# Two cross-attention layers with layer norm: d spread by two transfers through DRAM, the variance from ScalarE's squares, x's blocks in 4 transfers, new orders of work

## The reference

```
q = x Wq + bq          k = ctx Wk + bk          v = ctx Wv + bv
w = softmax over the 224 rows of x of (q k^T / sqrt(512))
y = w v + x
out = (y - mean(y)) / sqrt(var(y) + 1e-6) * gamma + beta       (over the 512 columns)
```

## Time and profile before

| What | Value |
|---|---|
| median of 3 runs | 1051.82 us |
| profiled execution | 1052.02 us, span 1050.1 us |
| PE busy | 1013.1 us, 96% of the span |
| PEld busy | 950.3 us, 90% |
| DVE busy | 867.4 us, 83% |
| ACT busy | 668.7 us, 64% |
| POOL busy | 563.3 us, 54% |
| DMA queue of SP | 99.02 MB, 43.8% of 16 engines |
| bv_row load on SP, issue to landing (median of 2) | 5.0 us |
| DVE waiting for the landing of cb before turn_ctx | 4 times, 2.4 us in all, longest 0.8 |
| ACT_TABLE_LOAD | once, 1.3 us |

### The profile page before, as it was taken

The page is one execution under the profiler, slowest core; times in us unless marked ns, Lnnn a source line. Parts: engine busy times, 40 slices in busy tenths (PEclk is TensorE's granted clock), DMA queues, the critical chain, the costliest instruction groups (busy, mean ns, idle before and its releaser), DMA issues.

```text
span 1050.1 us, 24861 instructions
## 1 busy us (share of the span) xinstructions
PE 1013.1 (96%) x6984; PEld 950.3 (90%) x6984; DVE 867.4 (83%) x2595; ACT 668.7 (64%) x1873; POOL 563.3 (54%) x517
## 2 busy tenths in 40 slices
PE   6888999999999999999999999999999999999984
PEld 5877999999999999999999999999999999999973
DVE  2465888888988888898898888998898889888864
ACT  2325676666666766767667766676677667666643
POOL 0013455665556556655556566555565665555653
PEclk9688999999999999999999999999999999999997
DMA  7743444444544443445444444454444444544101
GB/s 160 162 102 69 84 101 102 89 89 100 109 91 103 103 100 84 91 98 110 90 103 104 97 90 85 97 110 91 102 104 98 94 82 99 108 94 97 48 18 35
DMA packets 391214, 99.59 MB, mean 95 GB/s; under 512 B 324992, under 2 KB 375040, under 8 KB 391168
## 3 DMA queue, kind: packets, MB, share of 16 engines
q1 hardware_dynamic: 388528, 99.02, 43.8%
q10 hardware_dynamic: 2640, 0.01, 0.2%
HBM read 84.29 MB, written 14.68 MB: 94 GB/s over the span
## 4 chain that ended last, share of the span: by engine, by line
PE 91%; DVE 2%; issue 2%; POOL 2%; ACT 2%; SPq 1%; DMA 1%; POOLq 0%; DVEq 0%; ACTq 0%
PE oq_bank L599 26%; PE score_bank L575 8%; PE score_bank L576 8%; PE score_bank L580 8%; PE pv_bank L630 5%; PE pv_bank L625 5%; PE oq_bank L551 5%; PE pv_bank L626 5%; PE oq_bank L546 5%; PE oq_bank L547 5%; PE t_bank L511 3%; PE oq_bank L605 2%; PE pv_bank L457 1%; PE t_bank L528 1%; DMA y<-in_L_xattn_Wq_dram 1%
## 5 line engine op out<-in xcount | busy, mean ns | idle before, releaser
L599 PE MATMUL oq_bank<-probs,raw 125*128 125x224 f32 x1536 | 317.3, 357 | 5.2 <-ACT probs L766 5.2
L599 PEld LDWEIGHTS oq_bank<-probs,raw 125*128 125x128 f32 x1536 | 284.4, 192 | 7.7 <-ACT probs L766 3.6
L757 ACT ACTIVATE probs<-probs,neg_max 125x224 f32<-125x224 f32 x384 | 180.6, 471 | 141.9 <-DVE neg_max L967 141.8
L1151 POOL TENSOR_TENSOR psum<-probs 125x672 f32<-125x672 f32 x64 | 103.2, 1612 | 308.5 <-ACT probs L766 308.4
L575 PE MATMUL score_bank<-qT_hi,cT_hi 128*125 128x224 f32 x768 | 200.2, 287 | 3.0 <-ACT cT_hi L714 1.6
L576 PE MATMUL score_bank<-qT_hi,cT_lo 128*125 128x224 f32 x768 | 189.8, 273 | 0.0
L766 ACT ACTIVATE probs<-probs,rsum 125x224 f32<-125x224 f32 x384 | 153.3, 471 | 14.2 <-DVE rsum L975 12.7
L1194 POOL TENSOR_TENSOR y_out<-z,gamma_row 112x512 f32<-112x512 f32 x62 | 93.3, 1525 | 115.6 <-ACT z L790 115.6
L575 PEld LDWEIGHTS score_bank<-qT_hi,cT_hi 128*125 128x125 f32 x768 | 145.9, 190 | 7.4 <-issue 2.9
L580 PE MATMUL score_bank<-qT_lo,cT_hi 128*125 128x224 f32 x768 | 147.3, 273 | 0.0
L576 PEld LDWEIGHTS score_bank<-qT_hi,cT_lo 128*125 128x125 f32 x768 | 146.1, 190 | 0.0
(11 more groups left out here) (100 smaller groups left out, 2078.6 us busy)
## 6 DMA issues: line engine op xcount, KB each, us to landing
raw<-in_ctx_dram SPq DMA_DIRECT2D x64, 375.0 KB
cb<-in_ctx_dram SPq DMA_DIRECT2D x256, 92.0 KB
xb<-in_x_dram SPq DMA_DIRECT2D x512, 28.0 KB, 1.7
x<-in_x_dram SPq DMA_DIRECT2D x32, 448.0 KB, 3.6
out_dram<-y_out SPq DMA_DIRECT2D x31, 448.0 KB, 6.5
cb<-in_ctx_dram SPq DMA_DIRECT2D x128, 3.5 KB
y<-in_L_xattn_Wq_dram SPq DMA_DIRECT2D x2, 512.0 KB, 5.3
Wq_next<-in_L_xattn_Wq_dram SPq DMA_DIRECT2D x2, 512.0 KB, 5.8
```

The source lines that it names most:

```text
L599: ins = nc.tensor.matmul(o, raw[0:MP, u.slot, c, cols], probs[0:MP, u.par4, c, :], start=(c == 0), stop=(c == MC - 1))
L757: ins = act.activation(probs[0:MP, u.par4, c, :], probs[0:MP, u.par4, c, :], ACT.Exp, bias=neg_max[0:MP, u.par4, c:c + 1], scale=-1.0, acc ...
L1151: pool.tensor_tensor(psum3[0:MP, :, :], probs[0:MP, u.par4, 0:HALF, :], probs[0:MP, u.par4, HALF:MC, :], ALU.add).then_inc(psum3_done, 1)
```

## The change

The change has five parts.

- `spread_d` leaves TensorE and `d_out` leaves ScalarE. On SP, `save_d` writes `d_col` (112 partitions by 2 values of 4 bytes) to a DRAM tensor `d_kept`, and `spread_d` reads it back to 125 partitions of `d_row`, 224 values on each, when the first transfer has landed. `d_col` and `d_row` have two buffers, by parity of the unit.
- The mean is taken from the sum that `add_pv` now gives as a by-product (tensor_tensor_reduce); `minus_mean` (VectorE) scales it; `squares` (ScalarE) squares y minus the mean with the sum as accumulator output; `add_eps` and `shift` work on these. bn_stats and bn_aggr are gone.
- `load_xb` has 4 transfers of 112 KB.
- `transpose_x` waits for the low parts of the unit before, not for d.
- The orders of all five engines are new. TensorE's turn now begins with `q_product(a(+0), 0)`. SP's turn begins with the d of the last `b`.

```diff
-        XB_DMAS, CB_DMAS = P // RB * EC, P // RB * (LC + 1)
+        XB_DMAS, CB_DMAS = P // RB, P // RB * (LC + 1)
...
-                blocks = x[u.batch()].rearrange("(c r) (k b s) -> b k r c s", r=RB, k=EC, s=RB)
+                blocks = x[u.batch()].rearrange("(c r) (k b s) -> b r k c s", r=RB, k=EC, s=RB)
                 for b in range(P // RB):
-                    for k in range(EC):
-                        sp.dma_start(xb[b * RB:(b + 1) * RB, k, :, :], blocks[b, k]).then_inc(xb_loaded, 16)
+                    sp.dma_start(xb[b * RB:(b + 1) * RB, :, :, :], blocks[b]).then_inc(xb_loaded, 16)
...
+            def save_d(u):
+                if not u.real:
+                    return
+                if u.past(-2):
+                    sp.wait_ge(d_done[u.layer], u.batch(16))
+                    sp.sem_inc(wait_alone, 1)
+                sp.wait_ge(dot_done, u.n(m=2))
+                sp.sem_inc(wait_alone, 1)
+                sp.dma_start(d_kept[u.par].rearrange("(h p) -> p h", h=TH), d_col[0:TP, u.par, :],
+                             allow_slow_non_contiguous=True).then_inc(d_saved[u.layer], 16)
+            def spread_d(u):
+                if not u.real:
+                    return
+                if u.past(-2):
+                    sp.wait_ge(smax_done, u.n(-2, 6))
+                    sp.sem_inc(wait_alone, 1)
+                sp.wait_ge(d_saved[u.layer], u.batch(16, 16))
+                sp.sem_inc(wait_alone, 1)
+                sp.dma_start(d_row[0:MP, u.par, :], d_kept[u.par].partition_broadcast(MP)).then_inc(d_done[u.layer], 16)
...
             def turn(i, j):                      # SP
                 a, b = units(i, j)
+                save_d(b(-1))
+                spread_d(b(-1))
+                if a(-1).later(0):
+                    load_ctx(a(-1), 1)
                 if a(+0).later(1):
                     load_cb(a(+0))
+                save_d(a(+0))
                 if a(+1).later(1):
                     load_xb(a(+1))
+                spread_d(a(+0))
+                store(b(-2))
+                if a(+0).later(0):
+                    load_ctx(a(+0), 0)
                 if a(+1).later(1):
                     load_x(a(+1))
-                if a(+0).later(0):
-                    load_ctx(a(+0), 0)
-                    load_ctx(a(+0), 1)
-                store(b(-2))
...
             def turn(i, j):                      # TensorE, as it is after
                 a, b = units(i, j)
+                if j is None and i == 0:
+                    transpose_weights(0); fold_weights(0); fold_c(0); fold_w(0)
+                q_product(a(+0), 0)
+                pv_product(a(-1), 0)
+                pv_product(a(-1), 1)
+                q_product(a(+0), 1)
+                if j is None and i == 0:
+                    transpose_weights(1)
+                o_product(b(-1), 0)
                 score_product(a(+0), 0)
+                score_product(a(+0), 1)
                 o_product(b(-1), 1)
                 transpose_x(b(+0), 0)
                 score_product(a(+0), 2)
                 if j is None and i == 0:
                     fold_beta(); fold_weights(1); fold_c(1); fold_w(1)
+                pv_product(b(-1), 0)
                 transpose_x(b(+0), 1)
+                pv_product(b(-1), 1)
                 q_product(b(+0), 0)
                 q_product(b(+0), 1)
                 o_product(a(+0), 0)
                 score_product(b(+0), 0)
                 score_product(b(+0), 1)
+                score_product(b(+0), 2)
                 o_product(a(+0), 1)
...
+            def squares(u, h):                   # ScalarE
+                act.wait_ge(mean_done, u.n(m=2, add=h - 1))
+                act.activation(square_junk[0:TP, :], y[0:TP, u.par, h, :], ACT.Square, bias=neg_mean[0:TP, u.par, h:h + 1],
+                               accum_out=square[0:TP, u.par, h:h + 1]).then_inc(square_done, 1)
...
+                dve.tensor_tensor_reduce(y[0:TP, u.par, h, :], pv_bank[h][0:TP, :], y[0:TP, u.par, h, :], 1.0,
+                                         0.0, ALU.add, ALU.add, y_sum[0:TP, u.par, h:h + 1]).then_inc(y_done, 1)
+            def minus_mean(u, h):                # VectorE
+                dve.wait_ge(y_done, u.n(m=2, add=h - 1))
+                dve.tensor_scalar(neg_mean[0:TP, u.par, h:h + 1], y_sum[0:TP, u.par, h:h + 1], -1.0 / E, None,
+                                  ALU.mult).then_inc(mean_done, 1)
```

More of the change, by code:

```diff
@@ L150, in build_xattn @@
         qT_lo = sb("qT_lo", [P, LC, T], F32R)
-        d_col = sb("d_col", [P, TH])
-        d_row = sb("d_row", [P, T])
+        d_col = sb("d_col", [P, 2, TH])
+        d_row = sb("d_row", [P, 2, T])
         dot_junk = sb("dot_junk", [P, E])
@@ L729, in xT_hi_part @@
                 act.activation(xT_hi[:, u.par, 2 * g:2 * g + 2, :], src, ACT.Identity).then_inc(xT_hi_done, 1)
-            def d_out(u):
-                if not u.real:
-                    return
-                act.wait_ge(d_ready, u.n())
-                if u.past(-1):
-                    act.wait_ge(smax_done, u.n(-1, 6))
-                act.activation(d_row[:, :], t_bank[0][:, 0:T], ACT.Identity).then_inc(d_done, 1)
             def q_hi(u, l):
@@ L1050, in turn @@
                 a, b = units(i, j)
-                shift(b(-2), 0)
-                score_max(b(-1), 2)
+                add_pv(b(-2), 0)
+                invert_sum(a(-1), 1)
+                q_lo(b(-1), 0)
+                dot(a(+0), 1)
+                q_lo(b(-1), 1)
+                add_pv(b(-2), 1)
+                minus_mean(b(-2), 0)
+                minus_mean(b(-2), 1)
+                xT_lo_part(a(+0), 0)
+                turn_x(a(+0), 1)
+                score_max(b(-1), 0)
+                score_max(b(-1), 1)
+                score_max(b(-1), 2)
+                add_eps(b(-2))
+                xT_lo_part(a(+0), 1)
+                score_max(b(-1), 3)
+                turn_ctx(a(+0), 0)
+                invert_sum(b(-1), 0)
+                shift(b(-2), 0)
+                score_max(b(-1), 4)
+                o_lo(a(-1), 0)
+                ctxT_lo(a(+0), 0)
+                score_max(b(-1), 5)
+                turn_ctx(a(+0), 1)
+                o_lo(a(-1), 1)
                 shift(b(-2), 1)
-                dot(a(+0), 0)
-                dot(a(+0), 1)
                 residual(a(-1), 0)
                 residual(a(-1), 1)
-                score_max(b(-1), 3)
-                invert_sum(b(-1), 0)
-                o_lo(a(-1), 1)
-                score_max(b(-1), 4)
-                score_max(b(-1), 5)
-                ctxT_lo(a(+0), 0)
+                ctxT_lo(a(+0), 1)
                 add_pv(a(-1), 0)
                 q_lo(a(+0), 0)
-                turn_ctx(a(+0), 1)
                 invert_sum(b(-1), 1)
-                half_moments(a(-1), 0)
+                minus_mean(a(-1), 0)
+                turn_ctx(a(+0), 2)
                 add_pv(a(-1), 1)
-                half_moments(a(-1), 1)
-                moments(a(-1), 0)
-                moments(a(-1), 1)
-                ctxT_lo(a(+0), 1)
+                ctxT_lo(a(+0), 2)
                 q_lo(a(+0), 1)
@@ L1076, in turn @@
                     WqT_out(1)
+                minus_mean(a(-1), 1)
                 add_eps(a(-1))
-                turn_ctx(a(+0), 2)
+                turn_ctx(a(+0), 3)
+                score_max(a(+0), 0)
                 shift(a(-1), 0)
-                o_lo(b(-1), 0)
-                shift(a(-1), 1)
-                ctxT_lo(a(+0), 2)
-                score_max(a(+0), 0)
-                turn_ctx(a(+0), 3)
-                score_max(a(+0), 1)
-                ctxT_lo(a(+0), 3)
+                shift(a(-1), 1)
+                score_max(a(+0), 1)
+                score_max(a(+0), 2)
+                ctxT_lo(a(+0), 3)
+                score_max(a(+0), 3)
+                o_lo(b(-1), 0)
+                dot(b(+0), 0)
+                dot(b(+0), 1)
+                invert_sum(a(+0), 0)
+                o_lo(b(-1), 1)
                 xT_lo_part(b(+0), 0)
-                o_lo(b(-1), 1)
-                score_max(a(+0), 2)
-                score_max(a(+0), 3)
+                residual(b(-1), 0)
+                score_max(a(+0), 4)
+                residual(b(-1), 1)
                 if j is None and i == -1:
@@ L1109, in turn @@
                 xT_lo_part(b(+0), 1)
[L1110 to L1129 removed]
+                dot(a(+1), 0)
             turns(dve, turn)
```

187 lines of the change are left out of this document (73 added, 114 removed).

## The result

The changed kernel takes 1421.2 us (median of 4 runs, 1418.5 to 1423.6); the kernel before took 1050.6 in the same session. Ratio 1.3536, 95% interval 1.3516 to 1.3555: 35% slower. The forecast was 1055, range 1043 to 1071.

What follows compares the result with a forecast made beforehand. It took TensorE's own instruction list to bound the middle and chains of waits the two ends. Sum: 1052.0 - 9.7 (middle) + 0 + 12.7 (start) + 0.3 (end) = 1055.3, say 1055 us; range 1043 to 1071.

Steps and rivals of the forecast that it cites:

- Part 1: TensorE in the steady turn: without the two spread_d, 0.32 us saved a turn, 9.7 us in all.
- Part 2: Other engines in the steady turn: nothing becomes late, cost 0, range 0 to +15 us; tightest place q_lo(b,0).
- rival D: Engines at q_lo(b,0): the 0.5 us of slack is not there, 0.25 us a turn, 1063 us; chance 0.18.
- Rival E: ScalarE: Square needs another function table than Exp, four table loads a turn, 1112 us; chance 0.03.
- Part 3: SP's list in the steady turn: save_d lands in 2.0 us, waits covered, cost 0, up to 4 us a turn.
- rival C: SP's turn becomes the bound: spread_d(b) waits for save_d ahead of load_cb, 1071 us; chance 0.14.
- Part 4: The start: first d behind the preamble's loads, fold_beta +16.1 us, some regained; net +12.7, range +3 to +20.
- D: At the start, the time when the first unit's d lands: 56 us, from 46 up to 64.
- B: Rival at the start: preamble packets run denser, d lands near 47, net start +3, 1045 us; chance 0.18.
- Part 5: The end: last d's round trip hidden, last normalisation's mean and square cost +0.3 us, range -1 to +3.

Runs made afterwards that it cites:

- the floor: The changed kernel with no transfer of d in any turn, d_row filled once from a weights row in the preamble: 1037.8 us, 0.9884 of the kernel before.

## Why the prediction was wrong, by its own steps

**Part 1 was right.** The floor without transfers has a turn of (815.15 - 108.63) / 24 = 29.44 us; the same orders with two spreads on TensorE have (825.92 - 110.44) / 24 = 29.81. The difference is 0.37 for the 0.32 of the sum, and the two ratios, 0.9884 and 0.9982, differ by 10.3 us for its 9.7. The 0.12 from there to the 29.93 before would be 3.6 us, within the 5 us by which the kernel before varies from run to run.

```profile
108.63 2.28 PE oq_bank L590 x12
...
815.15 2.28 PE oq_bank L590 x12
```

**Part 2 was right.** In the floor TensorE waits once in 840 us, for 0.4 us, so the slack that rival D doubted is there. The whole floor is 11.8 us under the kernel before, where parts 1 and 2 gave 9.7. Rival E falls too: the trace of the changed kernel has one ACT_TABLE_LOAD, and its squares take 719 ns.

**Part 3 failed**, at this sentence: no such write is in the trace, "so I bound save_d by these 1.6 and 7.3 and take 2.0, near the median, since the queue is almost empty then". The write lands after 7.1. The nearest row was of another kind: xb's transfers read DRAM in pieces of 128 bytes. The bounds of 1.6 and 7.3 hold the median, though not the longest landing, 10.3; taking a value near the low end took the loss out of the forecast. The reason given, an almost empty queue, is refuted by the lone write on an idle core, 5.9 to 6.9 us. The Trainium skill, "DMA: Bandwidth & Descriptors", section "Anatomy of one DMA — SWDGE (gpsimd) path", with its fixed 2.0 us, gives the same sum; the trace disagrees for this write (7.1, and 7.8 where GpSimd issues it), and the lone transfers lie on both sides of it (1.15 for one row, 6.7 for d).

The high end was too small as well. I had "up to 4 us a turn", and for rival C one us a turn for each us beyond 2.5. At 7.1 that makes 7.1 - 2.5 - 0.8 = 3.8 a turn, times 31 and on top of 1055, 1173 us; it was 11.3 a turn. What C left out: the length of cb's issues, 14.2 us on the chain where the sum has 9, by the load of ctx's columns now ahead of them, the read and the write; and TensorE's lower clock behind the wait, about 2 us. 3.8, 5.2 and 2 are 11.0 of the 11.3, an estimate, since its terms come from different turns. In whole kernels the read was worth 83 us and the write's presence 133. SyncE's free time from xb's fewer issues was counted at 7 us from the 9.14 of the start; in steady turns the 16 issues took 7.8 before and the four take 3.0 without d's transfers, 4.8 us less, and behind save_d(a) they took 6.41.

So C had the right place, SyncE's list ahead of load_cb, and the right sign, with a chance of 0.14 and a price for one of its costs. Its sign, "load_cb's landing shows as a wait of DVE in every turn", is what the trace shows, 30 times.

**Part 4**: right mechanism, size off. D was 65.5 for 56, fold_beta 26.7 later for 16.1, and none of it came back: o_product of unit 2 is at 121.36 for 93.86, +27.5, where the sum had +12.7. The queue had been judged well: save_d was issued at 50.97 where the sum had 52. The miss is the round trip: 14.6 us (write landed at 61.3, d used at 65.59) where the sum had two landings of 2. B, a cheap start, falls. **Part 5** wasn't measured by itself. The chances at the end add up to 0.15 faster and 0.44 slower, not 0.16 and 0.43.

## What to carry to other kernels

Before a small value is sent through DRAM, price these things: the write's landing, the read's, the wait for each place where it stands in an ordered queue (nothing where other issues cover it), what the transfer does to the issues behind it, waited for or not, and what TensorE's lower clock adds behind the waits. A duration that no row shows needs the end that hurts as the working value when the queue behind it has loads with little slack. If such a round trip is needed, give each partition's values one piece and issue it from the list of an engine with a gap; here that took 1421 to 1072, and the spread on TensorE was still better at 1047. Pieces 32 bytes or more apart landed fastest alone (1.4 us), but no kernel was run with them. No version with d through DRAM beat the kernel before, and the new orders with d on TensorE are 0.2% below it, under the 0.5% that counts here.

## What the runs showed of the hardware that I had not expected

- Small writes to DRAM depend on the distance between pieces: 112 pieces of 4 bytes take 6.2 to 7.0 us side by side, 2.5 to 2.8 at 8 bytes, 1.4 at 32 and 64 bytes.
- Such a write can delay the issues behind it in its queue even if nobody waits: two issues of cb took 7.66 us for 5.32, with a load of 375 KB between the read and them. Without that load in between they took 0.89, behind a write that had landed.
- While cb was awaited TensorE was busy 2.6 of 6 us; then its granted clock was 0.50 for 13 us, and the first products behind the wait took 0.85 us for 0.45.
- score_max took the same 384 ns with its d operand in each second place of a row, and 549 ns in each fourth.
